# The feed of two units in eight of the second scan is made by GpSimd in SBUF instead of by VectorE in PSUM

## The reference, cut to what matters

```python
xs = jnp.concatenate([xp, xp[:, ::-1]], axis=0)
x_dbl = xs @ W_x
...
delta = jax.nn.softplus(dts + b_dt)

def step(hst, inp):
    d_t, u_t, B_t, C_t = inp
    dA = jnp.exp(d_t[:, :, None] * A)
    hst = dA * hst + (d_t * u_t)[:, :, None] * B_t[:, None, :]
    y_t = jnp.einsum('bdn,bn->bd', hst, C_t)
    return (hst, y_t)
...
y1, y2 = (ys[:M], ys[M:])
y = y1 + y2[:, ::-1]
```

## Time and profile before

| what | value |
|---|---|
| time, median of 3 runs | 1852.36 us (1852.25 to 1855.26) |
| time of the profiled execution | 1850.41 us |
| its span, first to last instruction | 1848.6 us |
| VectorE busy over the span | 1545.3 us (84%) |
| TensorE busy over the span | 1510.9 us (82%) |
| ScalarE busy over the span | 1199.0 us (65%) |
| GpSimd busy over the span | 1083.4 us (59%) |
| mean granted TensorE clock | 0.946 of full speed |

### The profile page before, as it was taken

One profiled execution on the slowest core, in us unless ns is written; L12 is line 12 of the kernel. 1 busy time (PEld: TensorE's weight loads), 2 busy tenths in 40 slices (PEclk: granted clock), 3 DMA queues, 4 the chain that ended last, 5 costly groups with the idle time before them and its releaser, 6 DMA issues. The chain is left out here.

```text
span 1848.6 us, 29091 instructions
## 1 busy us (share of the span) xinstructions
PE 1510.9 (82%) x9964; PEld 776.9 (42%) x9964; DVE 1545.3 (84%) x1266; ACT 1199.0 (65%) x1854; POOL 1083.4 (59%) x704
## 2 busy tenths in 40 slices
PE   6999897998778788878888778578888888888688
PEld 3666545886333333333333333225333333333223
DVE  3777655545899999999999999863899999999965
ACT  5666584335666677666766666367777776776456
POOL 1777401000477777777777777510698998999611
PEclk8999998999899999999999999889999999999989
DMA  5000000000354445544455444400000000000001
GB/s 151 2 0 0 1 1 1 1 1 1 58 103 91 91 91 96 95 92 91 91 96 95 92 91 91 87 15 4 1 1 1 1 0 0 0 0 0 1 8 46
DMA packets 23296, 77.97 MB, mean 42 GB/s; under 512 B 3776, under 2 KB 4672, under 8 KB 22976
## 3 DMA queue, kind: packets, MB, share of 16 engines
q0 software_dynamic: 18288, 66.59, 19.1%
q1 hardware_dynamic: 4944, 10.55, 2.0%
HBM read 8.45 MB, written 2.10 MB: 6 GB/s over the span
## 5 line engine op out<-in xcount | busy, mean ns | idle before, releaser
L1184 POOL TENSOR_TENSOR s_prod<-s_ahead,s_cs 128x1024 f32<-128x1024 f32 x127 | 308.8, 2432 | 184.1 <-DVE s_back L1127 155.9
L2076 POOL TENSOR_TENSOR r_state<-r_state,r_cs 128x1024 f32<-128x1024 f32 x127 | 301.0, 2385 | 116.5 <-ACT r_cs L1962 96.7
L2027 DVE TENSOR_TENSOR_SCAN r_state<-r_decay,r_pu 128x1024 f32<-128x1024 f32 x128 | 292.7, 2287 | 14.7 <-PE r_py L1878 9.6
L1124 DVE TENSOR_TENSOR_SCAN s_ahead<-s_fore,s_pu 128x1024 f32<-128x1024 f32 x128 | 292.7, 2287 | 8.5 <-ACT s_fore L1041 1.6
L1127 DVE TENSOR_TENSOR_SCAN s_back<-s_aft,s_pu 128x1024 f32<-128x1024 f32 x128 | 289.5, 2262 | 1.2 <-ACT s_aft L1051 1.2
L1946 ACT ACTIVATE r_decay<-r_pd,r_aneg 128x1024 f32<-128x1024 f32 x128 | 142.8, 1115 | 102.1 <-PE r_pd L1820 101.7
L1041 ACT ACTIVATE s_fore<-s_pd,s_aneg 128x896 f32<-128x896 f32 x128 | 129.9, 1015 | 112.7 <-PE s_pd L854 111.8
L1820 PE MATMUL r_pu<-r_partsu,selr 64*128 64x512 f32 x512 | 157.2, 427 | 23.6 <-DVE r_state L2027 20.8
L854 PE MATMUL s_pu<-s_partsu,selr 64*128 64x512 f32 x512 | 97.4, 459 | 80.5 <-DVE s_back L1127 77.0
L2023 DVE TENSOR_TENSOR r_pu<-r_pu,r_bs 128x1024 f32<-128x1024 f32 x128 | 154.7, 1208 | 8.3 <-PE r_pu L1820 8.2
L1820 PE MATMUL r_pd<-r_partsd,selr 64*128 64x512 f32 x512 | 157.7, 428 | 0.0
(11 more groups left out here) (356 smaller groups left out, 3267.7 us busy)
## 6 DMA issues: line engine op xcount, KB each, us to landing
s_ahead<-s_back POOLq DMA_DIRECT2D x127, 512.0 KB, 4.5
x_act<-in_x_dram SPq DMA_DIRECT2D x8, 256.0 KB, 5.6
out_dram<-x_act SPq DMA_DIRECT2D x16, 128.0 KB, 2.3
k_fir<-in_pack_fir_dram SPq DMA_DIRECT2D x1, 1600.0 KB, 7.7
k_scan<-in_pack_scan_dram SPq DMA_DIRECT2D x1, 1600.0 KB, 11.1
k_l<-in_pack_l_dram SPq DMA_DIRECT2D x1, 515.0 KB, 4.7
k_l<-in_pack_l_dram SPq DMA_DIRECT2D x1, 450.0 KB, 11.8
k_ln<-in_pack_ln_dram SPq DMA_DIRECT2D x3, 131.0 KB, 2.1
```

The source lines that it names most:

```text
L1124: dve.tensor_tensor_scan(ahead[:, v % 4], f, feed[:], 0.0, ALU.mult, ALU.add).then_inc(ahead_done, 1)
L1184: pool.tensor_tensor(prod[:, b], ahead[:, v % 4], cs[:, buf].rearrange("p i n -> p (i n)"), ALU.mult).then_inc(prod_done, 1)
L2027: dve.tensor_tensor_scan(state[:, v % 4], decay[:, v % 4], feed[:], 0.0, ALU.mult, ALU.add).then_inc(scanned, 1)
L2076: pool.tensor_tensor(state[:, v % 4], state[:, v % 4], cs[:, phase, q // 2], ALU.mult).then_inc(multiplied, 1)
```

## The change

In the units whose number in the group of eight is 0 or 2 (`by_pool`), but not in the first unit of all, VectorE no longer multiplies u by B. ScalarE copies u from `ps_u[0]` to the SBUF tile `back[v % 4]`, which is not yet in use for this unit; GpSimd multiplies that tile by B in place; ScalarE copies it back into `ps_u[0]`; and VectorE's scans read the feed from there as before. On ScalarE the first copy stands ahead of the decays of the same unit, and the second at the end of the step's copies of B or C, ahead of the work for the next block. On GpSimd the feed's product stands ahead of the step's product with C, and in such a step the adding DMA is issued first of all, behind a wait for the last sum of the even units and a product on a tile of one column (`tick`). The semaphores `u_copied`, `pool_fed` and `returned` rise by 4 per pooled unit; `fed` rises by 2 at the unit after a pooled one, so that its count stays that of the units. VectorE waits for the copy of B in the units 1 and 3 too, since it no longer did so in 0 and 2.

```diff
+        u_copied, pool_fed, returned = m.sem("s_ucop"), m.sem("s_poolfed"), m.sem("s_returned")
+        tick = m.sb("s_tick", [P, 1])
...
+        def by_pool(p, v):
+
+            return v % 8 in (0, 2) and live(p, UNITS) and not (isinstance(p, int) and p < 2)
+
+        def pooled(p, v):
+
+            return p + v % 8
...
+                if by_pool(p, v):
+                    act.wait_ge(u_rep, p + 1)
+                    wait(act, summed[0], 8 * p - 16)
+                    act.activation(back[:, v % 4], ps_u[0][:], ACT.Copy).then_inc(u_copied, 4)
                 if live(p, UNITS):
                     b, g = v % 2, place(v)[2]
                     act.wait_ge(d_ps, p + 1)
...
                 states(1)
+                if by_pool(p, v):
+                    act.wait_ge(pool_fed, pooled(p, v))
+                    act.activation(ps_u[0][:], back[:, v % 4], ACT.Copy).then_inc(returned, 4)
...
                 if live(p, UNITS):
                     b, buf = v % 2, v % 4 // 2
-                    dve.wait_ge(u_rep, p + 1)
-                    if v % 2 == 0:
-                        dve.wait_ge(b_copied, p + 2)
+                    f, a = fore[:, b].rearrange("p n t -> p (n t)"), aft[:, b].rearrange("p n t -> p (n t)")
                     feed = ps_u[b]
-                    dve.tensor_tensor(feed[:], feed[:], bs[:, buf].rearrange("p i n -> p (i n)"),
-                                      ALU.mult).then_inc(fed, 1)
-                if live(p, UNITS):
-                    f, a = fore[:, b].rearrange("p n t -> p (n t)"), aft[:, b].rearrange("p n t -> p (n t)")
-                    dve.wait_ge(fed, p + 1)
+                    if by_pool(p, v):
+                        dve.wait_ge(returned, pooled(p, v))
+                    else:
+                        dve.wait_ge(u_rep, p + 1)
+                        if v % 2 == 0 or v % 8 in (1, 3):
+                            dve.wait_ge(b_copied, p - v % 2 + 2)
+                        dve.tensor_tensor(feed[:], feed[:], bs[:, buf].rearrange("p i n -> p (i n)"),
+                                          ALU.mult).then_inc(fed, 2 if by_pool(p - 1, v - 1) else 1)
+                        dve.wait_ge(fed, p + 1)
                     dve.wait_ge(fore_done, p + 1)
                     wait(dve, prod_done, p - 3)
...
                 if live(f, UNITS - 1):
                     pool.wait_ge(ahead_done, f + 1)
                     pool.wait_ge(back_done, f + 1)
+                n, w = s - LAG_D, u - LAG_D
+                feeds = by_pool(n, w)
+
+                def add():
+                    pool.dma_start(ahead[:, z % 4], back[:, z % 4], accum_op=ALU.add).then_inc(summed[z % 2], 16)
+
+                if feeds:
+                    if live(f, UNITS - 1):
+                        wait(pool, summed[0], 8 * f)
+                        pool.tensor_tensor(tick[:], tick[:], tick[:], ALU.mult)
+                        add()
+                    pool.wait_ge(b_copied, n + 2)
+                    pool.wait_ge(u_copied, pooled(n, w))
+                    pool.tensor_tensor(back[:, w % 4], back[:, w % 4], bs[:, w % 4 // 2].rearrange("p i n -> p (i n)"),
+                                       ALU.mult).then_inc(pool_fed, 4)
                 if live(p, UNITS - 1):
...
                     pool.tensor_tensor(prod[:, b], ahead[:, v % 4], cs[:, buf].rearrange("p i n -> p (i n)"),
                                        ALU.mult).then_inc(prod_done, 1)
-                if live(f, UNITS - 1):
-                    pool.dma_start(ahead[:, z % 4], back[:, z % 4], accum_op=ALU.add).then_inc(summed[z % 2], 16)
+                if live(f, UNITS - 1) and not feeds:
+                    add()
```

More of the change, by code:

```diff
@@ L1166, in _ @@
         def _(pool):
+            pool.memset(tick[:], 0.0)
             pool.memset(fore[:, :, :, 0:1], 0.0).then_inc(zeroed, 1)
```

## The result

The changed kernel takes 1873.27 us (median of 4 runs, 1872.16 to 1881.89) against 1853.81 before (4 runs): a ratio of 1.0115, 95% interval 1.0091 to 1.0139. It is slower by a little over 1%, as forecast (1873.5).

The account below looks back on a forecast made before the run. VectorE was taken to set the pace of the second scan; late forward scans, 7 x 1.15 + 7 x 1.75 = 20.3 plus about 1, gave +21 us: 1871.4 on the profiled execution, 1873.5 us as median, range 1863 to 1892.

Parts of the forecast that it names:

- What the chain waits for: Second scan, pooled units: VectorE's forward scan waits for GpSimd's product with C, queued behind the feed product; break-even 6.86 us.
- The signs named beforehand: Second scan: 97 feed products on VectorE, 31 on GpSimd, 62 copies; idle before forward scan 8.5 to some 66 us.
- Its prices: Durations in the pooled feed's chain: copy about 1.02 us, GpSimd product 2.35, hand-over between engines 0.15.
- The estimate of 2.25: GpSimd product by the Trainium skill's 4497 ns for 2048 columns: 2.25 us, making the sum some 5 us smaller.
- Unit 0 and unit 2: Pooled units, quick case: forward scans begin 7.02 and 7.85 us after the previous feed product, 0.16 and 0.99 late.
- quick group: Group of eight units with TensorE's clock 1.00 in unit 0's step; 7 of 14, costing 1.15 us each.
- slow-clock case: Seven of 14 full groups with ScalarE later, six at clock 0.70: units begin at 7.42 and 8.31, costing 1.75 us each.
- The sum: Second scan: 7 x 1.15 + 7 x 1.75 = 20.3, and about 1 us more: +21 us.
- about 1 us: Addition to the sum for unit 2 of the first group and for the last group, without softplus chain in front.
- Costed at nothing: Second scan: earlier adding DMA, tick, later GpSimd products, larger fed increments, b_copied waits and ScalarE/TensorE lag, all given no cost.
- the rival in which they become the bound: ScalarE and TensorE fail to recover their lag, each group growing by up to 4 us: about 1912 us; 12%.
- The faster rival: Copy back, not the C product, releases the forward scan; starts at 5.9 and about 6.7, about 1836 us; 7%.

Follow-up runs that it names:

- the product first: Changed kernel with GpSimd's product with C moved ahead of the feed's product, no tick, adding DMA last: 1859.20 us, ratio 1.0037 to the kernel before.
- its eight relatives: The eight follow-up kernels, each an edit of the changed kernel's order, pooled units or feed use: 1849.79 to 1883.48 us.
- unit 2 alone: Changed kernel with only unit 2 of each eight pooled, unit 0 not: 1875.75 us, ratio 1.0130 to the kernel before.
- the Exp moved in the changed kernel's order: Changed kernel with ScalarE's softplus Exp issued behind the copy of u in unit 2's step: 1869.51 us, ratio 1.0095 to the kernel before.

## Why the prediction was right

**What the chain waits for.** Right, and shown: reversing the two GpSimd products changes the releaser and takes two thirds of the loss away, and VectorE, given its 37.5 us of products back, does all but about 2 of them within the wait. The rest of the loss is another wait: with the product first, ScalarE's copy back ends 43.8 of the 49.4 us that are left. The signs named beforehand came as well: 97 products on VectorE, 31 on GpSimd and 62 copies, and 61.2 us of idle time before the forward scan, where some 66 were forecast.

**Its prices.** The copy was put at 1.02 us, and measured 1.025 out of PSUM and 1.022 into it; a GpSimd product at 2.35, and the starts 1022.50 and 1024.84 are 2.34 apart; the hand-over at 0.15, and 1021.30 + 1.03 to 1022.50 is 0.17. The estimate of 2.25 came from the 4497 ns for 2048 columns in the GPSIMD Engine Reference of the Trainium skill, which stands in its section 3.1 (Elementwise — side-by-side cycle accounting); by it the loss would have been 5 to 6 us smaller, and the measured 2.36 decides. By section 4.1 (Engine selection) of the same page of the Trainium skill, GpSimd is about half as fast as VectorE at such work; the trace agrees, with 2.36 us against 1.21. That speed alone does not settle the sign here, though: unit 0 with the product first gained.

**Unit 0 and unit 2.** Forecast at 7.02 and 7.85 in a quick group, and found at 7.15 and 7.75 in one kind of group. In the other kind unit 0 was at 6.98, against 7.04. The prediction took that 7.04 for a part of the slow-clock case, and this was a misreading: before the change, four groups at full clock have it, and three at the lower clock have 6.87. In the two changed groups with a clock of 0.70, unit 2 began at 8.13 and 8.23, where 8.31 was forecast, and unit 0 at 7.40 and 6.99, where 7.42 was.

**The sum.** Here three terms were off, and not all in one sense. The slow-clock case was given 7 of 14 groups, as before the change; it came in 2, some 3 us less. A quick group was put at 1.15, which one kind of group cost; the other cost 0.79, 1.7 us less in all. And the first group's unit 2, part of "about 1 us", cost 2.6: the first four gaps add to 30.80 us in place of 28.22. From the first to the last forward scan the change costs 739.52 - 721.73 = 17.8, where 21 was forecast. The span grew by 21.7; the other 3.9 lie before the first and after the last forward scan, where the change adds nothing but the clearing of the tick's tile. The time from the last forward scan to the end was 662.3 us before and 659.5 to 666.9 in the changed kernel and its eight relatives, so this part can't be told from scatter. That the forecast came out to 0.3 us is luck; the 17.8 is what the mechanism can be held to.

**Costed at nothing.** The tick took 0.19 us and the adding DMA was issued by 1021.79, before the wait for the copy ended. Units 1 and 3 to 7 of the full groups keep gaps of 5.62 to 5.71, so the lag that unit 2 leaves on ScalarE and TensorE is made up within the group; the rival in which they become the bound didn't come.

**The faster rival.** Its mechanism is real but not in this kernel: with the product first, the copy back does release the scan, yet for unit 0 at 6.3 to 6.8 and for unit 2 at 7.25 to 7.79, not at the 5.9 and 6.7 that the rival gave. Only unit 0 gains.

## What to carry to other kernels

Work taken off the busiest engine pays only if the detour ends before that engine wants the result. Follow the detour from the moment its input may exist (here the end of the scan that frees the PSUM bank), and count on each engine what stands ahead of it in the queue and also what now stands behind it: here two thirds of the cost sat in a product that the new instruction had pushed back, not in the new instruction. Choose the places by slack of the helping engines, unit by unit; one unit in eight, with GpSimd's old order kept, gained 0.2%, where two in the new order lost 1.2%.

## What was not expected of the hardware

TensorE's granted clock in unit 0's step is not the same in every group, though the instructions are. Two full groups of the changed kernel, each with unit 7's step and the step of unit 0 behind it (columns as above, the clock third from the end):

```profile
598.90:604.50 5.60, 3.56 (x28) 1.72 (x28) 5.57 (x4) 2.95 (x4) 4.51 (x3) 1.00 0.62 117
604.60:610.20 5.60, 4.89 (x28) 2.43 (x28) 5.48 (x4) 3.93 (x6) 3.98 (x4) 0.70 0.68 129
1014.50:1020.10 5.60, 4.94 (x28) 2.41 (x28) 5.57 (x4) 2.98 (x4) 4.49 (x3) 0.70 0.60 113
1020.10:1025.70 5.60, 4.07 (x29) 2.10 (x30) 5.57 (x4) 4.55 (x7) 4.28 (x4) 1.00 0.68 129
```

So the clock falls in both groups, part of the time to 1.2 in place of 2.4 GHz, but in one in unit 0's step and in the other one step ahead, where the same 28 matmuls then take 4.94 us in place of 3.56. All 14 full groups of the changed kernel are of these two sorts: 2 have the 0.70 in unit 0's step, 12 in unit 7's. Before the change it stood over unit 0's step in 6, over unit 7's in 7, and over neither in one. Just before the matmuls of u TensorE had stood idle for 2.07 us or more in the groups of the first sort, and for 0.70 to 1.50 in those of the second.

Over unit 0's step a clock of about 0.7 or less stood in 8 of 14 groups with unit 2 alone, and in 6 with the Exp moved in the changed kernel's order. In the run with unit 2 alone, unit 2 begins at 7.52 to 7.68 in the groups at full clock and at 8.20 to 9.39 in the others. Before the change the forward scans began no later for it. What decides between the two steps stays open: no run here was made to tell that, and with one trace for each kernel it isn't shown that the edits do.
